# A Macaron block on one core: the sums of the scan evacuated by ScalarE and gated later, and a slot of its own for the first tile's k

## What is computed

```python
x = x + 0.5 * stack(layernorm(x))
x = x + mamba(layernorm(x))
x = x + 0.5 * stack(layernorm(x))
```

```python
u     = silu(causal_conv(u0)); dt, Bm, Cm = split(u @ x_proj_w)
delta = softplus(dt @ dt_w + dt_b)
s     = exp(delta * A) * s + (delta * u) * Bm      # 256 channels x 16 states, step by step
y     = sum_n(s * Cm) + u * D
out   = (y * silu(res)) @ out_w + x
```

## Time and profile before

| | before |
|---|---|
| median of 3 runs | 3350.98 us |
| the profiled execution | 3348.16 us, span 3346.4 us |
| PE, DVE, ACT, POOL busy, share of the span | 95%, 84%, 75%, 73% |
| first stack, Mamba layer, second stack | about 1530, 280 and 1535 us |
| the scan loop in it | 1583.0 to 1812.7 us |
| PE's share of the chain that ended last | 39%, "issue" 4%, DVE 3%, POOL 2%, ACT 2% |

### The profile page before, as it was taken

One profiled execution on the slowest core, in us unless ns is written; L12 is line 12 of the kernel. 1 busy time (PEld: TensorE's weight loads), 2 busy tenths in 40 slices (PEclk: granted clock), 3 DMA queues, 4 the chain that ended last, 5 costly groups with the idle time before them and its releaser, 6 DMA issues.

```text
span 3346.4 us, 120438 instructions
## 1 busy us (share of the span) xinstructions
PE 3190.6 (95%) x51618; PEld 2522.9 (75%) x51618; DVE 2794.2 (84%) x3204; ACT 2504.1 (75%) x3163; POOL 2438.6 (73%) x1233
## 2 busy tenths in 40 slices
PE   7999999999999999998888899999999999999999
PEld 5888888887887887874333788888888878788777
DVE  7888888888888888877897888888888888888886
ACT  5777777777777777777675677777777777777776
POOL 6777777777776776763898777777768768768764
PEclk8999999999999999999999999999999999999999
DMA  3333333233233332221000332323323323323322
GB/s 113 89 76 87 75 83 88 68 90 85 67 89 84 73 83 65 71 72 60 1 0 0 86 76 69 93 68 83 91 65 88 88 69 86 91 71 80 74 64 69
DMA packets 142299, 245.22 MB, mean 73 GB/s; under 512 B 32397, under 2 KB 34638, under 8 KB 141774
## 3 DMA queue, kind: packets, MB, share of 16 engines
q1 hardware_dynamic: 141774, 237.51, 27.9%
HBM read 35.01 MB, written 1.05 MB: 11 GB/s over the span
## 4 chain that ended last, share of the span: by engine, by line
PE 39%; issue 4%; DVE 3%; POOL 2%; ACT 2%; DVEq 0%; POOLq 0%; ACTq 0%
PE PS L270 7%; PE PS L390 6%; PE PS L214 4%; PE PS L410 4%; PE PS L216 3%; PE PS L215 3%; PE PS L331 3%; PE PS L527 2%; ACT ARENA L912 1%; DVE ARENA L1619 1%; PE PS L474 1%; PE PS L475 1%; PE PS L476 1%; POOL ARENA L1806 1%; PE PS L433 1%
## 5 line engine op out<-in xcount | busy, mean ns | idle before, releaser
L1695 POOL TENSOR_TENSOR ARENA<-ARENA,RN 128x1024 f32<-128x1024 f32 x192 | 365.4, 1903 | 456.5 <-ACT RN L902 456.5
L270 PE MATMUL PS<-C,ARENA 128*128 128x128 f32 x4608 | 613.5, 276 | 34.4 <-ACT ARENA L912 16.3
L1687 POOL TENSOR_TENSOR ARENA<-ARENA 128x1024 f32<-128x1024 f32 x192 | 468.4, 2439 | 233.9 <-DVE ARENA L1284 233.0
L270 PEld LDWEIGHTS PS<-C,ARENA 128*128 128x128 f32 x4608 | 512.0, 141 | 111.0 <-issue 76.6
L214 PE MATMUL PS<-WL,XH 128*128 128x512 f32 x1152 | 490.0, 425 | 14.0 <-DVE ARENA L1284 7.5
L965 ACT ACTIVATE ARENA<-PS 64x1024 f32<-64x1024 f32 x384 | 390.2, 1016 | 98.0 <-PE PS L270 94.7
L1681 POOL TENSOR_TENSOR ARENA<-ARENA 128x1024 f32<-128x1024 f32 x192 | 458.0, 2385 | 6.5 <-DVE ARENA L1269 6.4
L216 PE MATMUL PS<-WH,XH 128*128 128x512 f32 x1152 | 455.3, 395 | 0.0
L215 PE MATMUL PS<-WH,XL 128*128 128x512 f32 x1152 | 453.4, 394 | 0.0
L390 PE MATMUL PS<-ARENA 128*64 128x64 f32 x12288 | 401.1, 224 | 40.7 <-DVE ARENA L1322 24.5
L390 PEld LDWEIGHTS PS<-ARENA 128*64 128x64 f32 x12288 | 376.1, 138 | 75.8 <-issue 75.8
(11 more groups left out here) (155 smaller groups left out, 6493.9 us busy)
## 6 DMA issues: line engine op xcount, KB each, us to landing
ARENA<-ARENA SPq DMA_DIRECT2D x1152, 128.0 KB, 2.4
ARENA<-ARENA SPq DMA_DIRECT2D x768, 64.0 KB, 2.1
ARENA<-in_wqkv SPq DMA_DIRECT2D x36, 512.0 KB, 4.9
ARENA<-in_wo SPq DMA_DIRECT2D x12, 512.0 KB, 3.9
ARENA<-in_w SPq DMA_DIRECT2D x12, 341.0 KB, 4.0
ARENA<-in_w SPq DMA_DIRECT2D x12, 192.0 KB, 3.9
X<-in_xT SPq DMA_DIRECT2D x4, 256.0 KB, 5.0
out<-X SPq DMA_DIRECT2D x1, 768.0 KB, 3.5
```

The costliest lines, as they stand in the source:

```text
L270: last = nc.tensor.transpose(PS[:, slot, 128 * j:128 * j + 128], src[:, 128 * j:128 * j + 128], ident)
L1687: nc.gpsimd.tensor_tensor(KN[n % 2], KN[n % 2], T2, ALU.add).then_inc(k_add, 1)
```

## The change

Scan loop:

- D's product moves from `accumulate(k)` with n = 0 to after the products with n = 7.
- A new step on ACT, `keep_sums(h)`, in step k % 16 = 1, copies the two banks of sums as they are to Y (semaphore m_yc). The next chunk's first `accumulate` waits for these copies. DVE's gate becomes one product Y = Y * RES in place, in step k % 16 = 4 between the two scans (m_yg). `mamba_out` and ACT's copy of it move from k % 16 = 5 and 6 to 9 and 10. The last chunk keeps a gate that reads PSUM (`gate_last`).

A stack's entry:

- k of tile 0 is projected into slot 1 and squared into SB, a buffer of the softmax. It waits for `scale_in(1)` and no more for q's rotation, the third `scale_in` or four `keep_clock` products. q of tile 1 waits for the rotation of q of tile 0 alone. `carry(0)`, which writes slot 1, waits for the rotation of k of tile 0. k of tile 1 has three `keep_clock` products before it, not four, and these use bank 5.
- In the second stack `mamba_residual(3)` stands before `q_sums(0)` and no more before `k_rotate2(0)`.

```diff
@@ q_project(n), n == 1
                     if r == 1:
-                        pe.wait_ge(m_yd, 8)
+                        pe.wait_ge(m_yg, 4)
                         mamba_out(pe, 3, 7)
                     mean_in(pe, r, 3)
-                    keep_clock(2)
+                    pe.wait_ge(i_done, 4 * r + 3)
+                    keep_clock(2, 5)
+                    pe.wait_ge(q_rot, n0 + 1)
+                    project(1, 0, 0, q_done)
+                    return
@@ k_project(n)
-                if n < 2:
-                    keep_clock(4)
+                if n == 1:
+                    keep_clock(3, 5)
                 pe.wait_ge(x_lo, N // 4 * r + n // 4 + 1)
                 pe.wait_ge(w_lo[1], l0 + n // NT + 1)
+                if n == 0:
+                    pe.wait_ge(i_done, 4 * r + 2)
+                    project(0, 1, 1, k_done)
+                    return
@@ carry(n), n == 0
                     pe.wait_ge(pad_set, r + 1)
+                    pe.wait_ge(k_rot, n0 + 1)
@@ tensor_stack, loop over s
-                if s == 19:
-                    pe.wait_ge(i_done, 4 * r + 3)
@@ accumulate(pe, k)
             if k == 0:
                 pe.wait_ge(m_dl, 4)
-                pe.wait_ge(m_dg, 1)
             elif n == 0:
-                pe.wait_ge(m_yd, 2 * h)
+                pe.wait_ge(m_yc, 2 * h)
             for b in range(2):
-                if n == 0:
-                    nc.tensor.matmul(PSB[:, 6 + b, :], DG[:, 128 * b:128 * b + 128], UC[:, h, b, :], start=True, stop=False,
-                                     skip_group_check=True)
-                last = nc.tensor.matmul(PSB[:, 6 + b, :], ident, PR[k % 2][:, b, :], start=False, stop=n == 15,
+                last = nc.tensor.matmul(PSB[:, 6 + b, :], ident, PR[k % 2][:, b, :], start=n == 0, stop=n == 15,
                                         skip_group_check=True)
             last.then_inc(m_y, 1)
+            if n == 7:
+                pe.wait_ge(m_dg, 1)
+                for b in range(2):
+                    nc.tensor.matmul(PSB[:, 6 + b, :], DG[:, 128 * b:128 * b + 128], UC[:, h, b, :], start=False, stop=False,
+                                     skip_group_check=True)
@@ tensor_mamba, loop over k
-                if 0 <= h < 3 and k % 16 == 5:
+                if 0 <= h < 3 and k % 16 == 9:
@@ mamba_out
-            pe.wait_ge(m_yd, 2 * c + 2)
+            pe.wait_ge(m_yg, c + 1)
@@ q_square(n)
-                if n:
+                if n == 1:
+                    act.wait_ge(q_ss, n0 + 1)
+                elif n:
                     act.wait_ge(k_ss, n0 + n)
@@ k_square(n)
-                act.wait_ge(q_ss, n0 + n + 1)
-                act.activation(SQ, PS[:, 0, :], ACT.Square).then_inc(k_sq, 1)
+                if n:
+                    act.wait_ge(q_ss, n0 + n + 1)
+                act.activation(SQ if n else SB, PS[:, 0 if n else 1, :], ACT.Square).then_inc(k_sq, 1)
@@ scalar_mamba
+            def keep_sums(h):
+                act.wait_ge(m_y, 16 * h + 16)
+                for b in range(2):
+                    act.activation(Y[:, h, b, :], PSB[:, 6 + b, :], ACT.Copy).then_inc(m_yc, 1)
...
-                if k > 16 and k % 16 == 6:
+                if k > 16 and k % 16 == 10:
...
+                if k > 1 and k % 16 == 1:
+                    keep_sums(k // 16 - 1)
@@ vector_stack
+                if n == 0 and r == 1:
+                    mamba_residual(dve, 3, 7)
                 dve.wait_ge(q_sq, n0 + n + 1)
...
-                if s == 18 + 1 and r == 1:
-                    mamba_residual(dve, 3, 7)
@@ vector_mamba, loop over k
-                if h >= 0 and k % 16 == 1:
-                    gate_out(dve, h)
+                if h >= 0 and k % 16 == 4:
+                    dve.wait_ge(m_yc, 2 * h + 2)
+                    nc.vector.tensor_tensor(Y[:, h, :, :], Y[:, h, :, :], RES[:, h, :, :], ALU.mult).then_inc(m_yg, 1)
                 scan(k, 1)
```

More of the change, by code:

```diff
@@ L175, in build @@
             "dt", "min", "ex", "sp", "dl", "du"))
-        m_bc, m_bev, m_cs, m_pr, m_dg, m_y, m_yd, m_out, m_done = (sem("m_" + n) for n in (
-            "bc", "bev", "cs", "pr", "dg", "y", "yd", "out", "done"))
+        m_bc, m_bev, m_cs, m_pr, m_dg, m_y, m_yc, m_yg, m_out, m_done = (sem("m_" + n) for n in (
+            "bc", "bev", "cs", "pr", "dg", "y", "yc", "yg", "out", "done"))
         m_da, m_db, m_sc = ([sem(f"m_{n}{b}") for b in range(2)] for n in ("da", "db", "sc"))
@@ L217, in project, with keep_clock @@
                 last.then_inc(done, 1)
-            def keep_clock(k, bank=3):
+            def keep_clock(k, bank):
                 for _ in range(k):
@@ L1277, in k_rotate1 @@
                     dve.wait_ge(kT_done, n0 + n - 1)
-                nc.vector.tensor_tensor(halves(KN[n % 2]), halves(PS[:, 0, :]), table(n, 2), ALU.mult)
+                nc.vector.tensor_tensor(halves(KN[n % 2]), halves(PS[:, 0 if n else 1, :]), table(n, 2), ALU.mult)
             def k_rotate2(n):
@@ L1283, in k_rotate2 @@
                 dve.wait_ge(q_add, n0 + n + 1)
-                nc.vector.tensor_tensor(halves(T2), halves(PS[:, 0, :])[:, :, ::-1, :], table(n, 3),
+                nc.vector.tensor_tensor(halves(T2), halves(PS[:, 0 if n else 1, :])[:, :, ::-1, :], table(n, 3),
                                         ALU.mult).then_inc(k_rot, 1)
@@ L1301, in k_sums @@
                 dve.wait_ge(k_sq, n0 + n + 1)
-                nc.vector.tensor_reduce(SS[:, n % 2, 16:32], heads(SQ), AX.X, ALU.add).then_inc(k_ss, 1)
+                nc.vector.tensor_reduce(SS[:, n % 2, 16:32], heads(SQ if n else SB), AX.X, ALU.add).then_inc(k_ss, 1)
             def floor_sums(n):
@@ L1434, in vector_stack @@
             if r == 1:
-                gate_out(dve, 3)
+                gate_last(dve)
             nc.vector.memset(B[64:128, 0:1], 0.0).then_inc(edge_set, 1)
@@ L1631, in vector_mamba, with gate_last @@
                     input_step(2 + k // 16)
-                if h >= 0 and k % 16 == 1:
-                    gate_out(dve, h)
+                if h >= 0 and k % 16 == 4:
+                    dve.wait_ge(m_yc, 2 * h + 2)
+                    nc.vector.tensor_tensor(Y[:, h, :, :], Y[:, h, :, :], RES[:, h, :, :], ALU.mult).then_inc(m_yg, 1)
                 scan(k, 1)
-        def gate_out(dve, h):
-            dve.wait_ge(m_y, 16 * h + 16)
+        def gate_last(dve):
+            dve.wait_ge(m_y, 64)
             for b in range(2):
-                nc.vector.tensor_tensor(Y[:, h, b, :], PSB[:, 6 + b, :], RES[:, h, b, :], ALU.mult).then_inc(m_yd, 1)
+                last = nc.vector.tensor_tensor(Y[:, 3, b, :], PSB[:, 6 + b, :], RES[:, 3, b, :], ALU.mult)
+            last.then_inc(m_yg, 1)
         def mamba_residual(dve, c, bank):
@@ L1728, in pool_stack @@
             if r == 1:
-                pool.wait_ge(m_yd, 8)
+                pool.wait_ge(m_yg, 4)
                 pool.wait_ge(m_out, 3)
```

## The result

The changed kernel took 3359.86 us (median of 9 runs, 3356.56 to 3362.67) against 3350.44 for the kernel before (9 runs, 3344.45 to 3351.74): ratio 1.0033, 95% interval 1.0024 to 1.0041. Forecast were 3349.1, a range of 3342.5 to 3357.5, and no difference that a measurement can tell. It is 9.4 us slower, and above the range. The profiled execution took 3359.86, its span 3358.1.

A forecast was written before the change was run, and what follows sets the result against it. The scan loop was taken as POOL's work plus POOL's waits, the stacks as full on PE. Loop +3.6 (-1.6 - 4.0 + 6.0 + 3.2) and entries -5.5 give -1.9 from 3350.98: 3349.1 us, range 3342.5 to 3357.5.

The forecast's parts named there:

- (a) Start: Scan loop's start: D's matmuls leave accumulate(0), so its burst halves and POOL waits less; -1.6 us (0 to -3.1).
- (b) Chunk ends: Scan loop, k = 17, 33, 49: ACT copies the sums in time and POOL's 1.32 us wait goes, three times; -4.0 us.
- (c) Gates: Scan loop, k = 20, 36, 52: the SBUF-only DVE gate costs POOL 2.0 us each; +6.0 us (3 to 10).
- the turn of k = 24: Input step at k = 24: DVE went when POOL's read_out ended, POOL's next drive stretched; POOL lost 2.0 us, assumed per gate.
- the bound of 3.3: Upper end of POOL's loss per gate, from the input step of k = 8, where POOL's drive went first: 3.25 us.
- the bad turn: Gates lose their turn as at k = 8, POOL's drive going first; part of the port and clock rival, chance 0.15.
- port and clock together: Rival, scan loop gates: DVE loses its turn and PE's clock falls, 4.65 us per gate; +8, total 3357; chance 0.15.
- (d) D's pair and mamba_out: Scan loop: D's matmuls add 1.7 us at k = 41 and 57, -0.25 at k = 25; +3.2 us (0 to 4.5).
- the cover that I counted on: At k = 25 the input step of k = 24 has DVE 2.4 us late, half covering the pile; wait 2.4, not 2.69.
- Entries: Both stack entries: earlier projection of tile 0's k brings q_rotate2(1) forward, -1.9 and -3.6 us; -5.5 in all (0 to -6).
- the case that I priced at -2.5: Entries: floor_sums(0) comes behind POOL's addition and q_rotate1(1) is late; gains fall to -2.5 and -0.8 us.
- I take the clock as it was: Entries: PE's clock assumed unchanged despite a wait before k1's projection; at worst each entry gives 2.4 us back.

The follow-up runs named there:

- gate_with_psum_input: The changed kernel with the gate's first input read from decay in PSUM, not the sums in SBUF (outputs differ); ratio 0.9992 to the kernel before.
- gate_k2: The changed kernel with the gate at k = 18, 34, 50 in place of 20, 36, 52; ratio 1.0011 to the kernel before.
- entries_again: The kernel before with only the change's two stack entries (three clock-keepers), run once more beside an eight-keeper version; ratio 1.0000 to the kernel before.
- entries_only: The kernel before with only the change's two stack entries, its scan loop left as before; ratio 0.9996 to the kernel before.
- loop_only: The kernel before with only the change's scan loop, both entries left as before; ratio 1.0028 to the kernel before.
- more_keepers: The changed kernel with eight clock-keeping products in place of three before tile 1's k is projected, both stacks; ratio 1.0021 to the kernel before.

## Why the prediction was wrong, step by step

**(a) Start, -1.6.** Right: -1.9.

**(b) Chunk ends, -4.0.** Right: -3.96, with ACT's copies where they were expected.

**(c) Gates, +6.0.** Here it failed. The mechanism was named, the port, but the sum took the turn of k = 24, 2.0 each. The step that failed is "the walk for k = 20 comes out with DVE waiting for the end of a read_out as at k = 24": I walked DVE's and POOL's instructions and not ACT's evacuation, which decides the turn by 0.06 us. It came out as k = 8 three times, 3.2 each in place of 2.0, inside the bound of 3.3. On top came 2.46 for the clock, less the 0.79 saved at k = 24: +11.3 in all. Two rows, one each way, were no ground for giving the bad turn 0.15, and the reason held against it, that PE would have less of a gap at k = 20, was wrong: 3.34 us there, 3.28 behind k = 8 in the kernel before. The rival "port and clock together" had 4.65 per gate, measured were 4.0, and its 3357 was 2.9 under the median.

**(d) D's pair and mamba_out, +3.2.** Right in kind, too small: +5.3. At k = 25 the cover that I counted on did not exist. POOL was waiting when the input step of k = 24 was issued, so the step took 1.20 and put DVE 1.2 late, not 2.4: 3.70 idle, not 2.4. (The sum there is also off by 0.4: its terms end at 1681.5, not near 1681.9.)

```profile
1671.32 1.20 DVE L1580 TENSOR_TENSOR ARENA<-ARENA 128x1024 f32<-128x1024 f32 x1
```

At k = 41 and 57 D's pair cost 2.15 in place of 1.7. In gate_with_psum_input, which has no slow accumulates ahead, it cost 1.7 (4.43 and 4.44 against 2.70), and as much in gate_k2 (4.44 twice), where the only ones ahead stood behind the gate of k = 34; that the other 0.45 comes from slow accumulates is likely and not shown. The mistake behind it is larger than the size. The same trace said that each gate leaves PE a gap of about 3 us; I never asked whether D's pair could stand in it. There it costs nothing.

**Entries, -5.5.** The chain was right to q_rotate2(1), -2.0 and -2.7 forecast as -1.9 and -3.6. floor_sums(0) came behind POOL's addition in the second stack and took 2.02, the case that I priced at -2.5. In seven of the nine kernels with these entries and three keepers it got in first (0.5 us), and q_rotate2(1) came 23.1 us behind the loop's end against 26.8 in the kernel before, which is all of the 3.6. "I take the clock as it was" is the step that failed: in the first stack the low clock took back 1.9 of the 2.0 us. In the traces, q_norm(2) of the first stack comes at 61.3 on the mean of nine kernels with the new entries and three keepers (59.5 to 63.1), against 62.1 for three with the old (61.8 to 62.6). In the second it comes 51.7 behind the loop's end (49.3 to 52.9) against 53.5 (51.1 to 56.7). That is 2.6 us for both, and 56.7, the row that I took my second entry from, was the worst of the three. The timed runs give 0 and -1.3 (entries_again and entries_only). Why q2 and v0 are slow in some executions and not in others stays open.

**The sum.** The loop was 7.2 us worse than forecast, the entries 3 to 5.5; that is the distance from -1.9 to +9.4, to within 2 us of one execution's chance. The chances were wrong with it. The four terms were taken as independent, yet a late gate gives the gap, the gap the clock, and both the lead that mamba_out then finds missing.

## What to carry to other kernels

Before an operation is moved onto a shared port, list for its new place what the other engine has ready at the moment of issue, with what releases each item, a third engine's included. A margin of a tenth of a microsecond is a coin toss: price both outcomes and arrange the order so that the good one has a wide margin. A gap made on PE is a place to put PE's loose work, which otherwise pays in full elsewhere and leaves the clock to fall. Where one profiled execution gives a term of the sum, look at how the same stretch differs in a second one before taking its slowest row as the thing to be won.

## What the runs showed of the hardware

A DVE product of 128x1024 with both inputs in SBUF, issued while POOL worked on SBUF operands, began when the running POOL instruction had ended and, behind it, whatever POOL had ready at the issue (times of the whole record, wait and product): none further at k = 18 (2.84 us), a drive at k = 20 (3.65), a drive and a read_out at k = 38 (5.36). With POOL idle at its issue it takes 1.20 to 1.21. While POOL was in a read_out, its drive went first if the releasing ACT instruction had ended at most 0.01 us behind DVE's issue, and DVE went first from 0.07 on. With POOL idle this does not carry over: at k = 24 of the changed kernel, loop_only and more_keepers the evacuation had ended 0.05 ahead, POOL's drive began 0.02 behind DVE's product, and it was the drive that took 2.30 in place of 1.3. The Trainium skill (SBUF — State Buffer, Who interferes with whom) says that the first to be issued has the port for its instruction; the runs agree, if an instruction that is ready in POOL's queue counts as issued. In the scan loop PE's granted clock fell behind every gate's gap of 3.33 to 3.35 us (nine in three kernels) and behind none of the gates' gaps of 1.43 (three). Of 15 gaps of 2.02 to 2.12 us in front of an accumulate, ten had a slow one behind them (2.6 to 3.7 us in place of 1.98) and five had not: a gap of that length is a toss too.
